# Turning, copying and scattering the last two expert groups of each stage tile by tile

## The reference

```python
x = x + 0.5 * ffn(layernorm(x))      # stage 1
x = x + attention(layernorm(x))
x = x + 0.5 * ffn(layernorm(x))      # stage 2

def ffn(x):                          # 64 experts, the best 8 for each token
    shared_out = swiglu(x, shared_w1, shared_w2)
    w_topk, idx_topk = top_k(softmax(x @ wg.T), 8)      # the 8 weights are normed to sum 1
    # each expert takes up to 160 of the tokens that chose it
    h = einsum('ech,efh->ecf', buf, expert_w1)
    x1, x2 = split(h, 2)
    out = einsum('ecf,ehf->ech', x1 * silu(x2), expert_w2)
    # each token adds up its 8 rows of out, with their weights
    return shared_out + combined
```

## Time and profile before

| | before |
|---|---|
| timed runs, median (lowest to highest) | 916.82 us (915.58 to 917.76) |
| span of the profiled execution, first to last instruction | 912.4 us |
| distance of the median from that span | 4.4 us |
| PE busy | 845.9 us (93%) |
| DVE busy | 568.7 us (62%) |
| ACT busy | 503.1 us (55%) |
| POOL busy | 492.2 us (54%) |
| scatters of stage 1 (L589) | 80, mean 995 ns |
| scatters of stage 2 (L1350) | 80, mean 1001 ns |

### The profile page before, as it was taken

One profiled execution on the slowest core, in us unless ns is written; L12 is line 12 of the kernel. 1 busy time (PEld: TensorE's weight loads), 2 busy tenths in 40 slices (PEclk: granted clock), 3 DMA queues, 4 the chain that ended last, 5 costly groups with the idle time before them and its releaser, 6 DMA issues.

```text
span 912.4 us, 18887 instructions
## 1 busy us (share of the span) xinstructions
PE 845.9 (93%) x6360; PEld 748.5 (82%) x6360; DVE 568.7 (62%) x1738; ACT 503.1 (55%) x1376; POOL 492.2 (54%) x536
## 2 busy tenths in 40 slices
PE   5989989999964899999999999999879999999968
PEld 4889989999963677777777777777679999999954
DVE  8947753333336877788888888877543385333337
ACT  4422333333322888888888888888732333333327
POOL 4156777777752222256666666666557254444440
PEclk9779999999996999999999999999999999999989
DMA  9947877777626890000000000000050688888648
GB/s 321 374 160 226 255 232 225 235 237 228 202 90 224 197 151 1 1 17 28 22 25 22 28 22 25 22 20 14 6 211 18 218 299 285 279 289 280 228 134 316
DMA packets 68479, 140.72 MB, mean 154 GB/s; under 512 B 10479, under 2 KB 37552, under 8 KB 68292
## 3 DMA queue, kind: packets, MB, share of 16 engines
q1 hardware_dynamic: 56644, 118.59, 40.0%
q0 software_dynamic: 11776, 21.39, 7.6%
HBM read 107.72 MB, written 35.56 MB: 157 GB/s over the span
## 4 chain that ended last, share of the span: by engine, by line
PE 51%; POOL 11%; ACT 11%; DVE 9%; issue 7%; DMA 4%; SPq 0%; DVEq 0%; ACTq 0%; POOLq 0%
PE ps L1370 12%; ACT at_prob L2255 7%; PE ps L615 7%; PE ps L1949 6%; PE ps L1389 6%; POOL y_rows L589 5%; POOL f_xg L578 5%; DVE at_nmax L2078 3%; PE ps L72 3%; PE ps L1990 2%; PE ps L655 2%; DMA f_yt<-y_rows 2%; PE ps L1975 2%; PE ps L1962 2%; ACT at_qkT L2249 2%
## 5 line engine op out<-in xcount | busy, mean ns | idle before, releaser
L1843 POOL TENSOR_TENSOR at_m<-at_m 128x512 f32<-128x512 f32 x64 | 81.4, 1272 | 146.4 <-DVE at_m L2071 146.4
L1181 POOL DMA_INDIRECT xs_rows<-xr,slots_of x128 | 127.2, 994 | 43.6 <-issue 32.0
L2255 ACT ACTIVATE at_prob<-ps,at_nmax 128x256 f32<-128x256 f32 x256 | 117.8, 474 | 39.5 <-DVE at_nmax L2078 39.0
L1350 POOL DMA_INDIRECT y_rows<-f_og,f_put x80 | 80.0, 1001 | 97.8 <-ACT f_og L1502 78.0
L878 DVE TENSOR_TENSOR f_ehid<-f_esil,ps 128x480 f32<-128x480 f32 (+1 forms) x80 | 50.7, 634 | 116.1 <-ACT f_esil L719 107.8
L1639 DVE TENSOR_TENSOR f_hid<-f_sil,ps 128x480 f32<-128x480 f32 (+1 forms) x80 | 50.6, 634 | 106.4 <-ACT f_sil L1495 99.8
L1370 PE MATMUL ps<-f_xgT,f_ring 128*128 128x160 f32 x768 | 115.0, 299 | 1.7 <-issue 1.7
L615 PE MATMUL ps<-f_xgT,f_ring 128*128 128x160 f32 x768 | 114.9, 299 | 0.2 <-issue 0.2
L719 ACT ACTIVATE f_esil<-ps 128x480 f32<-128x480 f32 (+1 forms) x80 | 44.3, 554 | 120.9 <-PE ps L615 120.9
L1495 ACT ACTIVATE f_sil<-ps 128x480 f32<-128x480 f32 (+1 forms) x80 | 44.3, 554 | 120.3 <-PE ps L1370 120.3
L1370 PEld LDWEIGHTS ps<-f_xgT,f_ring 128*128 128x128 f32 x768 | 107.0, 190 | 2.1 <-issue 2.1
(11 more groups left out here) (256 smaller groups left out, 1847.6 us busy)
## 6 DMA issues: line engine op xcount, KB each, us to landing
f_ring<-in_wexp SPq DMA_DIRECT2D x128, 576.0 KB, 5.0
y_rows<-zeros SPq DMA_DIRECT2D x16, 512.0 KB, 6.1
f_yt<-y_rows SPq DMA_DIRECT2D x16, 512.0 KB, 8.9
at_yt<-y_rows SPq DMA_DIRECT2D x6, 1024.0 KB, 4.9
xs_rows<-at_blank SPq DMA_DIRECT2D x16, 342.5 KB, 10.2
f_xg<-xs_rows SPq DMA_DIRECT2D x16, 342.5 KB, 3.4
y_rows<-f_og,f_put POOLq DMA_INDIRECT x160
y<-y_rows SPq DMA_DIRECT2D x4, 512.0 KB, 4.4
```

Of the source, the lines that this page charges most:

```text
L1181: nc.gpsimd.indirect_dma_start(xs_dram, bass.IndirectOffsetOnAxis(s.slots_of[:, t, k:k + 1], 0), s.xr[:, t, :], None, bounds_check=last_sl ...
L1843: nc.gpsimd.tensor_tensor(m1[:, p % 2, :], m1[:, p % 2, :], m2[:, p % 2, :], ALU.add).then_inc(msum, 1)
L2255: mm = nc.scalar.activation(prob[:, p % 2, h, t, :], ps[:, SB + h, t * SEQ:(t + 1) * SEQ], ACT.Exp, bias=nmax[:, p % 2, h, t:t + 1], accum ...
```

## The change

Groups 14 and 15 of both stages (the last step) are turned back, copied and scattered in four parts in place of two: tile 0, tile 1, tile 2, and tiles 3 and 4 together. A part stands as early as its tokens allow: tile 0 behind expert 1 (it needs expert 0), tile 1 behind expert 2, tile 2 behind expert 3, tiles 3 and 4 behind the first unit of the next group. For group 15, tile 2 stands ahead of expert 3's down projection, and tiles 3 and 4 behind it. The other 14 groups keep their two parts. `out_parts` and `parts_before` give the parts of a group and the count of parts ahead of it.

```diff
+def out_parts(G):
+    return ((0, 1), (1, 2), (2, 3), (3, GT)) if isinstance(G, int) and G >= EXPERTS // GE - STEP_GROUPS \
+        else ((0, 3), (3, GT))
+def parts_before(G):
+    return 2 * G if not isinstance(G, int) else sum(len(out_parts(k)) for k in range(G))
...
                         for c in range(GT):
-                            if c in (0, 3):
-                                pool.wait_ge(og_s, 2 * G + 1 + c // 3)
+                            if c in firsts:
+                                pool.wait_ge(og_s, parts_before(G) + 1 + firsts.index(c))
...
                     def turn_out(i, g, part):
                         G = SG * i + g
-                        pe.wait_ge(os_, unit(i, g, GE - 2 + part) + 1)
-                        after(pe, og_s, 2 * G + part)
-                        for s in range(3) if part == 0 else range(3, GT):
+                        a, b = out_parts(G)[part]
+                        pe.wait_ge(os_, unit(i, g, (b * P - 1) // CAPACITY) + 1)
+                        after(pe, og_s, parts_before(G) + part)
+                        for s in range(a, b):
...
+                            else:
+                                turn_out(i, g, 2)
                             down(i, u)
-                            if r in (0, 1) and not (first and g == 0):
+                            if not last and r in (0, 1) and not (first and g == 0):
                                 turn_out(*preceding(i, g), r)
-                            if last and g == SG - 1 and e in (GE - 2, GE - 1):
-                                turn_out(i, g, e - GE + 2)
+                            if last and g == 0 and r in (0, 1):
+                                turn_out(*preceding(i, g), r)
+                            if last and g > 0 and r == 0:
+                                turn_out(*preceding(i, g), 3)
+                            if last and e in range(1, GE) and u < len(todo) - 1:
+                                turn_out(i, g, e - 1)
+                            if last and u == len(todo) - 1:
+                                turn_out(i, g, 3)
...
                     def group_out(i, g, part):
                         G = SG * i + g
-                        act.wait_ge(og_t, 2 * G + part + 1)
+                        act.wait_ge(og_t, parts_before(G) + part + 1)
                         if part == 0:
                             after(act, sent[g], 16 * GT * i)
-                        a, b = ((0, 3), (3, GT))[part]
+                        a, b = out_parts(G)[part]
```

More of the change, by code:

```diff
@@ L584, in scatter @@
                             pool.wait_ge(zeroed, 16 * TILES)
+                        firsts = [a for a, _ in out_parts(G)]
                         for c in range(GT):
[L586 to L587 removed]
+                            if c in firsts:
+                                pool.wait_ge(og_s, parts_before(G) + 1 + firsts.index(c))
                             n = G * GT + c
@@ L745, in step @@
                                 silu(i + 1, 0)
-                            if r in (0, 1) and not (first and g == 0):
+                            if last and u == len(todo) - 1:
+                                group_out(i, g, 2)
+                            if not last and r in (0, 1) and not (first and g == 0):
                                 group_out(*preceding(i, g), r)
-                            if last and g == SG - 1 and e in (GE - 2, GE - 1):
-                                group_out(i, g, e - GE + 2)
+                            if last and g == 0 and r in (0, 1):
+                                group_out(*preceding(i, g), r)
+                            if last and g > 0 and r == 0:
+                                group_out(*preceding(i, g), 3)
+                            if last and e in range(1, GE) and u < len(todo) - 1:
+                                group_out(i, g, e - 1)
+                            if last and u == len(todo) - 1:
+                                group_out(i, g, 3)
                     for t in range(LEAD):
@@ L1410, in turn_out @@
                     G = SG * i + g
[L1411 to L1414, removed]
+                    a, b = out_parts(G)[part]
+                    pe.wait_ge(os_, unit(i, g, (b * P - 1) // CAPACITY) + 1)
+                    after(pe, og_s, parts_before(G) + part)
+                    for c in range(a, b):
+                        mm = nc.tensor.transpose(ps[:, GB, (c - a) * P:(c - a + 1) * P],
                                                  oT[:, g, c * P:(c + 1) * P], ident[:, :])
@@ L1434, in step @@
                                 up(*following(i, g), 0)
+                            else:
+                                turn_out(i, g, 2)
                             down(i, g, e)
-                            if e in (0, 1):
+                            if e in (0, 1) and not (last and g > 0):
                                 turn_out(*preceding(i, g), e)
-                            if end and e >= GE - 2:
-                                turn_out(i, g, e - GE + 2)
+                            if last and g > 0 and e == 0:
+                                turn_out(*preceding(i, g), 3)
+                            if last and e in range(1, GE) and not (end and e == GE - 1):
+                                turn_out(i, g, e - 1)
+                            if end and e == GE - 1:
+                                turn_out(i, g, 3)
                 shared_up(0, 0)
@@ L1497, in group_out @@
                 def group_out(i, g, part):
-                    act.wait_ge(og_t, 2 * (SG * i + g) + part + 1)
+                    act.wait_ge(og_t, parts_before(SG * i + g) + part + 1)
                     if part == 0:
                         after(act, sent[g], 16 * GT * i)
-                    a, b = ((0, 3), (3, GT))[part]
+                    a, b = out_parts(SG * i + g)[part]
                     nc.scalar.copy(og[:, g, a:b, :].rearrange("p c d -> p (c d)"),
```

2 lines of the change are left out of this document (1 added, 1 removed).

## The result

The changed kernel takes 909.97 us in the median of four runs (909.17 to 910.10), beside 916.20 for the kernel before on the same chip: ratio 0.9939, 95% interval 0.992 to 0.9959. That is 6.2 us between the medians; 6.0 were forecast. The profiled execution has a span of 907.4 us, 5.0 less than before.

A forecast was written before the change was run, and what follows sets the result against it. It took the stage ends to be bound by GpSimd's last scatters and, in stage 2, by group 14's landing, which starts the loads. Gains of 2.42 + 3.59 = 6.0 us took 916.82 to 910.8 us, range 909.3 to 913.8.

The forecast's parts named there:

- Stage 1: End of the first expert stage: group 15's last scatter starts earlier, so attention does too; 2.42 us, bounds 1.2 to 3.6.
- The Trainium skill's rule on the shared port: First stage's last two scatters might each wait up to 0.32 us for a vector operation, making the term 1.8 us.
- Stage 2, group 14: End of the second stage: group 14 lands earlier and the train of sixteen loads starts 3.59 us earlier (3.11 at least).
- the added wait: Second stage, group 14's first turn: TensorE waits 0.63 us, once, for ScalarE to copy a shared PSUM bank.
- Stage 2, group 15: Second stage: group 15 lands 2.25 us earlier, and the load train, started 3.59 us earlier, does not run dry.
- The first rival: Second stage bound by group 15's landing, gaining only 2.25 us there: 912.1 us; chance 0.08.
- ScalarE caught in stage 1: Group 14's tile 0 copy waits for group 12's landing and delays Silu, costing up to 7.8 us: 918.6; chance 0.05.
- Attention's clock: TensorE's clock in early attention rises late and costs 1.2 us of the first stage's gain: 912.0 us; chance 0.12.
- The sign that the prediction named: Prediction is wrong if first attention operation to start of the second expert stage gets longer by over 1 us.
- The sum: Whole kernel: 2.42 + 3.59 = 6.0 us, profiled span 912.4 to 906.4, median 4.4 us above it at 910.8.

The follow-up runs named there:

- e1: Stage 1 as changed, stage 2 with all groups in two parts as in the kernel before: ratio 0.9986 to the kernel before.
- e5: Changed kernel, but stage 2's group 14 in three parts, tiles 0 and 1 turned together behind expert 2: 909.03 us, ratio 0.9926 to the kernel before.
- e3: Changed kernel, but in stage 2 group 15 in two parts again, group 14 still in four: 912.58 us, ratio 0.9973 to the kernel before.
- e4: Changed kernel, but in stage 2 group 14 in two parts again and group 15 in three: 914.14 us, ratio 0.9986 to the kernel before.
- e2: Stage 2 as changed, stage 1 with all groups in two parts as in the kernel before: ratio 0.9966 to the kernel before.
- e10: The changed kernel measured again without any edit: 910.56 us, ratio 0.9945 to the kernel before.
- e6: Changed kernel, but stage 2's group 14 has its last part turned ahead of group 15's expert 0 down projection: 909.95 us, ratio 0.9941 to the kernel before.
- e11: The kernel of e7 measured again, beside e10 on one chip: 909.26 us, ratio 0.9932 to the kernel before.
- e7: Changed kernel with the edits of e5 and e6 together: 908.85 us, ratio 0.9924 to the kernel before.
- e9: Changed kernel, but in stage 1 group 14 in two parts again, group 15 still in four: 912.13 us in a single run.

## Why the prediction was right, step by step

*Stage 1.* The mechanism was right, and its size where nothing else came in: 2.42 us forecast, 2.37 in e1. In the profile after it was 1.71, for the gather's wait, which the prediction did not know and which comes and goes between profiles. Over the ten profiles with all of stage 1 changed the stretch has a mean of 35.06 us, against 37.22 in the two with stage 1 as before: 2.2 us.

*The Trainium skill's rule on the shared port* ("SBUF — State Buffer", "SBUF: two separate sides"), as the prediction applied it, is not seen here: the last two scatters ran beside the sixteen two-input sums (268.88 to 274.05) and took 0.98 us each, as the others did. The section's box on DMAs issued by GpSimd names vector operations in a 2-port mode, and one with two inputs in SBUF holds the ports, by the same section, only against a GpSimd operation that reads SBUF; no run tells which case this is.

*Stage 2, group 14.* Right: its last scatter was forecast 10.86 us after the turn and stood at 11.04. From copy to scatter it took 0.28 us (872.51 to 872.79), the lower end, as the single semaphore suggested. The first load came 3.40 us earlier, with 3.59 forecast; the difference is the added wait, which was sized 0.63 and measured 0.72, and 0.81 by e5. Its last piece, from the copy's end to the next transpose, was put at about 0.06 without a row, and took 0.15 (863.82 to 863.97).

*Stage 2, group 15.* This step was wrong in its reason. The prediction took the landing of 2.25 us, read where no loads ran, and put it where sixteen were under way: "the other eight are let go 7.8 us into it, with some five still under way. So no." They were let go 11.4 us into it (876.34 to 887.72) with three still to be summed, on the very edge. It was 5.6 us in the kernel before already. The waits of SyncE there show it: two waits for scatters of 15.5 us together, the longer 10.8 for group 14; the other 4.7 begins behind the eighth issue (885.94) and so ends at 890.6, with the last scatter at 885.01:

```profile
SPq L1311 <- DMA y_rows<-f_og,f_put: 15.5, 2, 10.8
```

The total was still right since group 15's own split brings its landing forward too. That it came level with the loads and not behind them is luck: the prediction had the late half let go 7.1 us before the eighth load is there (14.9 - 7.8), and it was 2.9 us before the eighth sum (24.69 to 27.61), with nothing to spare. The first rival (bound by group 15's landing) had 0.08; it is level with the forecast's case, and e3 shows it in full.

*ScalarE caught in stage 1* (the slower rival): the wait is there, and harmless as worked out. ScalarE's timeline of the changed kernel:

```profile
250.72 0.27 ACT L752 COPY f_og<-ps 128x128 f32<-128x128 f32 x1 [0.47 <-DMA y_rows<-f_og,f_put]
252.24 0.57 ACT L740 ACTIVATE f_esil<-ps 128x480 f32<-128x480 f32 x1 [1.25 <-PE ps L627]
```

*Attention's clock* (0.12). The rise from 0.50 to full speed does not keep its distance to the work. In windows of 1 us (length, busy times of PE, PEld, DVE, ACT, POOL, then the granted clock), the changed kernel:

```profile
289.00:290.00 1.00, 1.00 (x6) 1.00 (x5) 0.85 (x2) 0.37 (x1) 0.07 (x1) 0.50 0.96 397
290.00:291.00 1.00, 1.00 (x10) 1.00 (x9) 0.00 (x0) 0.55 (x1) 1.00 (x1) 0.88 0.05 16
```

and e4, whose attention starts within 0.1 us of the same time:

```profile
292.00:293.00 1.00, 1.00 (x7) 0.71 (x7) 1.00 (x2) 0.51 (x2) 0.00 (x0) 0.55 1.05 422
293.00:294.00 1.00, 1.00 (x11) 0.64 (x8) 0.34 (x2) 1.00 (x1) 0.81 (x1) 1.00 0.99 410
```

One rises within 290 to 291, the other within 292 to 293, with the same work. The first product with the values of attention comes 20.78 us after its first operation in the one and 21.91 in the other, so this costs up to 1.1 us. With all of stage 1 changed it comes after 20.78 to 21.97 us; in the two profiles with stage 1 as before, the kernel before (20.67) and e2 (20.83), it rose early. In the changed kernel this is 0.11 of the +0.67 us of the stretch. What made up the rest, between there and the first tokens turned in stage 2, I did not take apart; from those tokens to the turn both kernels take 167.02 us.

Nor is it shown that the change has no part in it. The whole stretch is 580.65 and 580.75 us in the two profiles with stage 1 as before, and 581.32 to 583.87 in the eleven with stage 1 changed, so a part of stage 1's gain may be lost there; two profiles, one of them of a quick execution, are too few to tell. The sign that the prediction named, over 1 us longer, is absent in the changed kernel's profile, but it stands in nine of the eleven (1.45 us in e1).

*The sum.* The span was forecast at 906.4 us and came out at 907.4: stage 1 gave 0.7 us less than its term, the stretch through attention took 0.7, and the end of stage 2 gave 0.3 more. The median is 0.8 us below the forecast all the same, since it lies 2.6 us above its profile and not 4.4 as before. The two misses pull opposite ways, and that the median comes so near is in part luck.

## What to carry to other kernels

A tail that is fed by two gates (first loads behind one group, later loads behind the next) moves in full only when both move: each group's split alone gave nothing or a third in stage 2, and group 15's alone gave nothing in stage 1. How near the two gates stand can differ between executions of one kernel, so one chain of waits does not settle which of them holds the end. Read a landing time at the place where it is used, beside the traffic that will be there; and when a chain is shortened, work out the second gate from its own rows, since it may already be level.

## What the runs showed of the hardware

The landing of a scatter of 64 KB depends on the loads beside it: 2.25 to 2.29 us without (once 2.9, in e10), 5.3 to 6.0 us beside the first eight loads of 512 KB (e6, e11, changed, e3, e7, e9), while GpSimd's own instruction stays at 0.98 to 1.11 us. TensorE's granted clock rises at different distances from the same work in profiles of kernels that do not differ there, which moves attention by about 1 us.
